# A two-layer metaformer on one core: the last phase's steps written out in a row, where 24 of its 33 stood in a loop of four units

## The reference, cut to what matters

```
x = x + L0_conv(ln_c(x))                 # 1x1 convolutions and clustering by similarity
t = tokens(x); t = t + L0_ffn(ln_t(t))   # 96 -> 384 -> 96, operands rounded to 8-bit floats
x = from_tokens(t)
x = x + L1_conv(ln_c(x))                 # fea = ln_c(x); n = layer norm of fea with gamma, beta
#   y = dw3x3(n); y = dw1x5(y); y = dw5x1(y); y = pw(y); L1_conv = y * n
t = tokens(x); t = t + L1_ffn(ln_t(t))   # h = relu(qlinear(ln_t(t), W1, b1)); qlinear(h, W2, b2)
return from_tokens(t)
```

## Time and profile before

| | |
|---|---|
| median of 3 runs | 4256.6 us (4250.14 to 4260.43) |
| the profiled execution, its own time | 4258.63 us |
| its span, first to last instruction | 4256.8 us |
| PE busy | 3309.3 us (78%) |
| DVE busy | 3027.4 us (71%) |
| ACT busy | 2686.4 us (63%) |
| POOL busy | 1408.0 us (33%) |
| last phase: first store of unit 0 to first store of unit 31 | 3089.18 to 4236.01 us |

### The profile page before, as it was taken

One profiled execution on the slowest core, in us unless ns is written; L12 is line 12 of the kernel. 1 busy time (PEld: TensorE's weight loads), 2 busy tenths in 40 slices (PEclk: granted clock), 3 DMA queues, 4 the chain that ended last, 5 costly groups with the idle time before them and its releaser, 6 DMA issues. The chain is left out here.

```text
span 4256.8 us, 81198 instructions
## 1 busy us (share of the span) xinstructions
PE 3309.3 (78%) x26660; PEld 2549.8 (60%) x26660; DVE 3027.4 (71%) x7852; ACT 2686.4 (63%) x5250; POOL 1408.0 (33%) x1892
## 2 busy tenths in 40 slices
PE   6767777676776777767669999999788777778787
PEld 5556555555555555555549999999544444444443
DVE  4888888888888888888842222222388788778787
ACT  2567667676676776766752222222388788888887
POOL 3555555555555555555310000000022221212221
PEclk8888788888888887888879999999799999999998
DMA  3133232332323323222146656656766565666562
GB/s 62 44 75 83 67 77 61 75 83 68 75 65 78 83 61 75 71 72 68 53 111 163 168 160 164 166 161 165 183 178 179 151 178 156 174 170 171 155 175 77
DMA packets 733857, 489.89 MB, mean 115 GB/s; under 512 B 420796, under 2 KB 712956, under 8 KB 721276
## 3 DMA queue, kind: packets, MB, share of 16 engines
q1 hardware_dynamic: 733564, 486.32, 43.3%
HBM read 284.42 MB, written 201.33 MB: 114 GB/s over the span
## 5 line engine op out<-in xcount | busy, mean ns | idle before, releaser
L1722 POOL TENSOR_SCALAR C_var<-C_st 128x16 f32<-128x16 f32 x64 | 13.2, 207 | 1775.8 <-DVE C_st L178 1775.8
L1264 PE MATMUL B_ps_row<-B_g,B_z 128*128 128x128 f32 x4608 | 555.8, 277 | 0.6 <-ACT B_g L1296 0.6
L1264 PEld LDWEIGHTS B_ps_row<-B_g,B_z 128*128 128x128 f32 x4608 | 532.2, 193 | 0.7 <-ACT B_g L1296 0.7
L178 DVE BATCH_NORM_STATS2 A_st<-A_xT 128x6 f32<-128x192 f32 x1536 | 446.7, 350 | 30.7 <-ACT A_xT L764 17.3
L166 POOL TENSOR_TENSOR A_rstd<-A_var,A_expo 128x16 f32<-128x16 f32 x128 | 454.2, 3549 | 23.8 <-POOL A_var L163 23.6
L1357 DVE TENSOR_TENSOR B_mid<-B_ps_row,B_row_bias 128x512 f32<-128x512 f32 x192 | 132.8, 692 | 457.7 <-PE B_ps_row L1264 447.7
L1394 ACT ACTIVATE C_q<-C_xT,C_shift,C_rstd 128x96 fp8e5<-128x96 f32 x1024 | 392.0, 457 | 41.5 <-POOL C_shift L1729 41.0
L307 ACT ACTIVATE A_h<-A_hid 128x1536 f16<-128x1536 f32 x256 | 370.6, 1448 | 55.4 <-PE A_hid L272 51.6
L307 ACT ACTIVATE C_h<-C_hid 128x1536 f16<-128x1536 f32 x256 | 370.5, 1447 | 20.0 <-PE C_hid L272 12.9
L794 ACT ACTIVATE A_xc<-A_xT,A_shift,A_rstd 128x96 f32<-128x96 f32 x1024 | 379.4, 462 | 0.0
L229 DVE TENSOR_SCALAR A_hq<-A_h,A_b 128x512 f16<-128x512 f16 x768 | 240.8, 369 | 178.9 <-ACT A_h L307 178.6
(11 more groups left out here) (162 smaller groups left out, 7778.4 us busy)
## 6 DMA issues: line engine op xcount, KB each, us to landing
A_xq<-in_x SPq DMA_DIRECT2D x32, 1536.0 KB, 8.9
x_scratch<-A_xT SPq DMA_DIRECT2D x64, 768.0 KB, 3.2
x_scratch<-A_x3h SPq DMA_DIRECT2D x64, 768.0 KB, 5.4
B_z<-x_scratch SPq DMA_DIRECT2D x96, 512.0 KB, 5.0
y_scratch<-B_y SPq DMA_DIRECT2D x96, 512.0 KB, 3.7
C_x3q<-x_scratch SPq DMA_DIRECT2D x32, 1536.0 KB, 9.2
C_y3q<-y_scratch SPq DMA_DIRECT2D x32, 1536.0 KB, 15.5
C_xT<-x_scratch SPq DMA_DIRECT2D x64, 768.0 KB, 14.7
```

Of the source, the lines that this page charges most:

```text
L178: return dve.bn_stats(st[:, n:n + 2, :].rearrange("p t s -> p (t s)"), x[:, n * C:(n + 2) * C].rearrange("p (t c) -> p c t", t=2))
L1264: m = pe.matmul(ps_row[h][:, b * P:(b + 1) * P], z[c.buf(NB)][:, h * HB + b, d:d + W], g[c.buf(2)][:, d, :], start=(d == 0), stop=(d == 2))
```

## The change

`steps` in `phase_c` no longer calls `sweep`. It calls `body` for each of the 33 steps with a constant unit, as `phase_a` does:

```
         def steps(eng, body):
-            sweep(eng, -1, 4, 6, 4, NQ - 1, NQ - 1, body)
+            for n in range(-1, NQ):
+                body(Unit(0, n, 4, NQ - 1))
```

## The result

The changed kernel takes 4210.56 us (median of 4 runs, 4210.38 to 4212.61), the kernel before 4258.52 us beside it. The ratio is 0.9891, with a 95% interval from 0.9874 to 0.9908: 1.1% less, between 39 and 54 us. A second series gave 4213.33 against 4255.41 us, ratio 0.9907 (0.9892 to 0.9922). The forecast was 4213.

What follows compares the result with a forecast made beforehand. DVE's fetch stalls at five jumps back were taken to bound the last phase: 4258.6 - 43.6, with 0 for register instructions and 0 for the longer stream, is 4215.0, less 2.0 for the median 4213 us; range 4204 to 4229.

Steps and rivals of the forecast that it cites:

- What bounds: Last phase: DVE's loop body doesn't stay resident, so five jumps back wait for fetches, 40.3 us, holding up PE and ACT.
- The sum: Whole kernel: 4258.6 less 43.6 us for five jumps gives 4215.0, then 4213 for the median.
- The other correction in the sum: Whole kernel: the median of the runs shown lies 2.0 us below the profiled execution, turning 4215.0 into 4213.
- The excess of 8.71 us: Last phase: steps with a jump average 44.30 us against 35.59 for ordinary ones; all of it comes off.
- the 0.65 us above DVE's wait: Five jump passages: 0.65 us each on top of DVE's 8.06 us wait, counted as saved too.
- Register instructions at 0: Last-phase loop: semaphore values worked out in registers are hidden behind the engines' work; removing them gains 0.
- The bound of 35.06 us from units 28 to 31: Last phase: fastest plain steps, 35.06 us against 35.33 in the loop, would give 5 us gained from register instructions.
- The longer stream at 0: Last phase, all five engines: fetching 24 more steps costs 0, since straight-line fetches are ahead of need.
- Half comes back through the clock: Last phase: all steps like units 12 to 15, 36.03 us with clock 0.95; 29.9 saved, 4227; chance 0.08.
- Slower through late fetches: PE's page crossings in the plain stream: about 33, at 2 us each the time is 4279; chance 0.05.
- it doesn't do what it seems: Last phase: the fetch is due anyway or another engine is late; 5 x 8 us stay, 4257; chance 0.03.
- The Trainium skill's figure for a branch: Last-phase jumps: about 108 ns each, six per engine are 0.6 us, so the change would do nothing measurable.

Runs made afterwards that it cites:

- the two runs that split the engines: Kernel before with only DVE's last-phase steps written out, 4209.39 us; kernel before with the other four engines written out and DVE looping, 4251.54 us.
- three jumps fewer: Kernel before with three rounds of the last-phase loop instead of six, units 16 to 31 plain: 4226.48 us, ratio 0.9941.
- DVE alone plain: Kernel before with only DVE's last-phase steps written out; PE, ACT, POOL and SP keep their loops: 4209.39 us, ratio 0.989.
- DVE alone in the loop: Kernel before with the last-phase steps of the other four engines written out, DVE keeping its loop: 4251.54 us, ratio 1.000.
- the first run: The changed kernel's first measurement against the kernel before: 4210.56 us, ratio 0.9891.
- the body 128 shorter: Kernel before, DVE's last-phase loop with bias and relu merged, line 233 and each group's second statistics instruction left out: 4149.09 us, ratio 0.9757.

## Why the prediction was right

**What bounds.** Right, and for the reason given: DVE's fetch at five jumps held PE and ACT up. That ACT and PE were only waiting was an argument from one timeline; the two runs that split the engines show it.

**The sum.** 43.6 us were expected. Between the stores it is 45.3 us in the first profile and 42.3 in the second, with 14 and 17 falls of the clock. The rest of the 47.9 us of the first profiled span is 2.9 us of clock at the phase's start, less 0.3 behind the last of these stores. So what the first profile gained beyond the sum is luck with the clock; the second profile has none of it, and the medians of that series lie 42.1 us apart. The other correction in the sum, 2.0 us between the profiled execution and the median, came from three runs; with the fourth it is 0.1. These small terms cancel in part, and that 4213 was met within 2.4 us is in part luck. The excess of 8.71 us was the right price, and taking it whole, with the 0.65 us above DVE's wait, too: three jumps fewer gave 27.3 us between the stores, 9.1 each.

**Register instructions at 0.** Right. With four engines plain and DVE in the loop nothing was gained, and ordinary steps in the loop and outside are 35.5 to 35.8 us. The bound of 35.06 us from units 28 to 31 was not a pace, though: the last of these three distances, 33.60 us, ends in step 31, which has no front half, and the other two are 35.07 and 36.51. Entering the loop does show, once: unit 3 to 4 takes 35.49 us with the clock at 1.00, 0.5 above a step without a fall. It is the same with DVE alone plain (35.50) and gone with DVE alone in the loop (35.00), so it is another engine's. It is too small to matter here.

**The longer stream at 0.** Right, though it was the term with the least behind it: only eight plain steps had been seen in this traffic. Queue 8 brings 30 packets in 740 us, one in 25, as the prediction had worked out. PE's longest wait on issue is 0.5 us, and ACT and DVE have none, so in a straight line the packets are there before they are needed.

**Half comes back through the clock.** It didn't: the mean of the steps hardly moved (35.59 us before, 35.53 and 35.63 after). Units 12 to 15, the model for this rival, were three steps in a row with a fall of the clock each. Such falls come in 14 and 17 of the 31 steps after the change, and came in 14 of the 26 ordinary ones before.

**Slower through late fetches** fell with the packets just named, and "it doesn't do what it seems" with the first run.

**The Trainium skill's figure for a branch**, about 108 ns for a compare-and-branch in "Advanced Engine Details and Errata", section "Control Flow Timing", comes without a condition. The run with the body 128 shorter is near it: its steps with a jump are 0.2 to 0.3 us longer than the others. It is no figure for a jump that has to fetch, 8.4 to 9.5 us here in the traffic of this kernel and 1.5 to 1.6 us without it.

**What was named wrongly** is the data that delay the fetch: the prediction pointed at C_xT, issued 1.1 us after the store, about when DVE jumps. It is x3 and y3, issued 5 us before the jump, and the fetch goes ahead of the last of them. The sum didn't hang on it.

## What to carry to other kernels

If steps of a loop come in two lengths, look whether the long ones are those that jump back, and whether an engine waits there on "issue" while an instruction packet comes: then its body is too long to stay, and each round pays a fetch that large loads in flight make about four times as long (8.1 us of waiting against 2.1 here). Write the steps out, shorten that one engine's body, or write out that engine alone (one engine of five gave the whole gain here); or at least have no large load in flight when it jumps. Loops with short bodies needn't be touched.

## What the runs showed of the hardware that was not expected

- Instruction fetches are delayed by data in the DMA queues: the wait at a jump is 2.0 to 2.3 us alone and 7.7 to 8.4 us with loads of 3 MB in flight. The packet starts in the midst of these loads, 5.2 to 5.9 us after DVE's last instruction, and not behind the last of them. Data that was issued about 1 us after the jump moved later than the packet.
- A DVE body of 386 records (by the trace) is fetched anew in each round, all five packets of it, and one of about 320 not at all. Of the two steps between, 64 instructions less left the price as it was, and 128 less took it away.
- Fetches of several engines at the same jump overlap: the excess is 9.5 us with PE, DVE and a third engine fetching, 8.7 with DVE alone.
- Short falls of the granted clock, in about half of the steps, cost about 1.2 us each in steps in which PE is 80% busy. With the body 128 shorter they come in whole stretches. These are windows over two stretches of that kernel, in which units took 32.5 and about 34.0 us: the granted clock is 1.00 in the one and 0.95 in the other.

```profile
3118.00:3215.00 97.00, 81.44 (x480) 47.18 (x479) 68.41 (x144) 91.99 (x169) 21.04 (x24) 1.00 0.71 196
...
3850.00:4050.00 200.00, 169.27 (x940) 98.36 (x939) 134.54 (x283) 181.43 (x329) 39.03 (x45) 0.95 0.67 185
```
